# Packed constant loads, contiguous input and output, and a new order of the first and last stage

## The reference

```
x = x + layernorm(mamba(layernorm(x)))       # in-projection, convolution, scan over 16 states, out-projection
x = x + layernorm(moe(layernorm(x)))         # 8 experts, top 2 of a softmax, and a shared ninth expert
x = x + layernorm(diff_attention(layernorm(x)))   # 8 heads, difference of two softmaxes, RMS norm
x = x + layernorm(ffn(layernorm(x)))         # attention whose q, k, v and output matrices are mixed from
                                             # 8 experts by a gate of each row, then a mixture of 8 experts
```

## Time and profile before

| what | us |
|---|---|
| median of 3 runs | 2786.39 |
| lowest and highest of them | 2784.11, 2788.78 |
| span of the profiled execution | 2789.0 |
| busy: PE | 2152.8 |
| busy: DVE | 2099.8 |
| busy: ACT | 1749.7 |
| busy: POOL | 1545.8 |
| share of the last chain on PE, DVE, ACT, issue, POOL | 34%, 30%, 12%, 12%, 11% |

### The profile page before, as it was taken

One profiled execution on the slowest core, in us unless ns is written; L12 is line 12 of the kernel. 1 busy time (PEld: TensorE's weight loads), 2 busy tenths in 40 slices (PEclk: granted clock), 3 DMA queues, 4 the chain that ended last, 5 costly groups with the idle time before them and its releaser, 6 DMA issues.

```text
span 2789.0 us, 42437 instructions
## 1 busy us (share of the span) xinstructions
PE 2152.8 (77%) x15570; PEld 1465.2 (53%) x15570; DVE 2099.8 (75%) x3549; ACT 1749.7 (63%) x2757; POOL 1545.8 (55%) x1375
## 2 busy tenths in 40 slices
PE   2333787588499597989889888989896699659876
PEld 1101455256266474655566566656664568546665
DVE  3999889789888315999999999999998531762344
ACT  5444776686575545988888888888894234222432
POOL 0435433533534103878877887888787524464146
PEclk8555898799599798999999999999997799879988
DMA  3000000000000000100000000111010000000000
GB/s 109 0 0 0 1 1 1 1 1 1 19 1 1 12 12 20 28 24 24 24 24 24 24 24 24 25 31 28 24 35 22 2 1 1 1 16 1 1 1 16
DMA packets 32033, 42.07 MB, mean 15 GB/s; under 512 B 8897, under 2 KB 18130, under 8 KB 31442
## 3 DMA queue, kind: packets, MB, share of 16 engines
q1 hardware_dynamic: 31826, 39.34, 5.2%
HBM read 12.05 MB, written 2.10 MB: 5 GB/s over the span
## 4 chain that ended last, share of the span: by engine, by line
PE 34%; DVE 30%; ACT 12%; issue 12%; POOL 11%; SPq 0%; DMA 0%; POOLq 0%; ACTq 0%; DVEq 0%
DVE MA L1330 12%; PE ps L892 6%; DVE WB L1339 5%; POOL MA L430 3%; PE ps L821 3%; ACT HR L793 2%; PE ps L1162 2%; PE ps L823 2%; PE ps L822 2%; PE ps L1191 2%; PE ps L2064 2%; ACT BIG L464 2%; PE ps L1174 2%; PE ps L2006 1%; ACT L793 1%
## 5 line engine op out<-in xcount | busy, mean ns | idle before, releaser
L1330 DVE TENSOR_REDUCE MA<-ps 128x1 f32<-128x1024 f32 x512 | 606.5, 1215 | 46.6 <-PE ps L1162 42.6
L1258 ACT ACTIVATE WB<-ps,MA 128x1024 f32<-128x1024 f32 x461 | 513.4, 1117 | 105.8 <-DVE MA L1330 93.5
L430 POOL TENSOR_TENSOR MA<-MA,BIG 128x1024 f32<-128x1024 f32 x128 | 303.0, 2389 | 494.9 <-DVE BIG L356 470.4
L1162 PE MATMUL ps<-BIG 96*128 96x512 f16 x1024 | 316.0, 391 | 98.7 <-ACT WB L1258 87.2
L1414 POOL TENSOR_SCALAR WB<-WB,MA 128x384 f32<-128x384 f32 x256 | 371.1, 1450 | 8.5
L892 PEld LDWEIGHTS ps<-WB,HR 128*128 128x128 f32 x2304 | 278.9, 195 | 27.4 <-issue 11.6
L892 PE MATMUL ps<-WB,HR 128*128 128x128 f32 x2304 | 285.9, 280 | 7.2 <-DVE acc L728 7.2
L793 ACT ACTIVATE HR<-ps,b 128x512 f32<-128x512 f32 x288 | 190.2, 686 | 127.7 <-PE ps L823 126.6
L1782 POOL TENSOR_TENSOR BIG<-MA,BIG 128x512 f32<-128x512 f32 x128 | 132.7, 1048 | 228.6 <-PE ps L2050 74.3
L1174 PE MATMUL ps<-ident,WB 128*128 128x128 f32 x1640 | 223.8, 280 | 9.8 <-DVE WB L1339 5.7
L1417 POOL TENSOR_TENSOR WB<-WB 128x384 f32<-128x384 f32 x205 | 208.9, 1019 | 17.1
(11 more groups left out here) (314 smaller groups left out, 4959.8 us busy)
## 6 DMA issues: line engine op xcount, KB each, us to landing
BIG<-BIG SPq DMA_DIRECT2D x192, 64.0 KB, 2.0
BIG<-MA SPq DMA_DIRECT2D x192, 64.0 KB, 2.0
WB<-w_dram SPq DMA_DIRECT2D x1, 2304.0 KB, 14.8
X<-x_dram SPq DMA_DIRECT2D x4, 512.0 KB, 12.5
HR<-w_dram SPq DMA_DIRECT2D x1, 2048.0 KB, 9.6
out_dram<-X SPq DMA_DIRECT2D x4, 512.0 KB, 3.2
BIG<-wqkv_dram SPq DMA_DIRECT2D x1, 1536.0 KB, 6.2
WB<-w_dram SPq DMA_DIRECT2D x2, 512.0 KB, 5.1
```

The costliest lines, as they stand in the source:

```text
L430: e.tensor_tensor(yy[:, c, :], yy[:, c, :], db[n % 2][c], ALU.add).then_inc(*p_my.up(b, n, c))
L1162: x = e.matmul(ps[s][:, 512 * h:512 * h + 512], stack[q % 2][0:96, 0, 2 * pp + s, 128 * i:128 * i + 128], stack[q % 2][0:96, 1, 2 * pp + s ...
L1258: e.activation(P_of(n, s), ps[s][:, :], ACT.Exp, bias=L[:, 2 * s + pp:2 * s + pp + 1], scale=1.0, accum_out=L[:, 4 + 2 * s + pp:5 + 2 * s ...
L1330: e.tensor_reduce(L_of(n)[:, c:c + 1], ps[s][:, :], AX, ALU.max, negate=True).then_inc(*v_amx.up(n, s))
```

## The change

Three things change together.

First, the loads. The host packs nine constants side by side into one array `first` of 128 x 1148 and ten others into `second` of 128 x 725 (values that were broadcast on the chip are now repeated on the host), and lays x out so that a partition's eight tiles lie in one row. SP issues x of batch 0, `first` and `second`, then the rest as before. `first` counts on `s_c`, `second` on a new semaphore `s_c2`. The output is stored in the same contiguous layout, and the host puts it back.

Second, the prologue. Selector block 1 goes from ACT to DVE, both of DVE's blocks come after the statistics instead of before them, and tiles 4 to 7 of batch 0 are normalized on DVE (new semaphore `v_mln`), tiles 0 to 3 on ACT.

Third, all the tables have new numbers, so instructions of the first stage, of the attention's edges and of the last stage stand in another order. The 256 units of the attention keep theirs.

```diff
+FIRST = (("ident", 128), ("winT", 512), ("convw", 6), ("convb", 2), ("bdt", 2), ("dcol", 2), ("alog", 32), ("wx", 208),
+         ("wdt", 256))
+SECOND = (("gwT", 8), ("b1", 36), ("gam", 1), ("sims", 16), ("woT", 256), ("iota8", 8), ("tri", 128), ("lam", 128),
+          ("gts", 16), ("b2", 128))
...
-OUT_AT = {"gate": 6.85, "yy": 4.84, "out": 11.16, "stats": 19.32, "rstd": 21.7, "norm": 32.4, "x": 35.2}
+OUT_AT = {'gate': 6.46, 'yy': 8.89, 'out': 9.57, 'stats': 16.28, 'rstd': 18.81, 'norm': 30.44, 'x': 35.17}
...
-        a_const = Tick(sem("a_const"), keys(("alog", "sel0", "sel1"), )  + keys(("w1",), 9) + [("gw",)])
-        v_const = Tick(sem("v_const"), keys(("aneg", "sel2"), ) + keys(("w1",), 9) + [("gw",), ("ones",)])
+        a_const = Tick(sem("a_const"), keys(("alog", "sel0"), )  + keys(("w1",), 9) + [("gw",)])
+        v_const = Tick(sem("v_const"), keys(("sel1", "sel2", "aneg"), ) + keys(("w1",), 9) + [("gw",), ("ones",)])
+        v_mln = tick("v_mln", ("in",))
...
         def const_act(e):
-            e.wait_ge(s_c, S_C)
...
+            e.wait_ge(s_c, 16)
+            e.activation(aneg[:, :], packed["alog"], ACT.Exp, bias=0.0, scale=1.0).then_inc(*a_const.up("alog"))
+            e.activation(*selected(0), ACT.Copy, scale=1.0).then_inc(*a_const.up("sel0"))
...
         def const_dve(e):
+            yield IN_AT0["stats"] + 1
+            e.wait_ge(s_c, 16)
+            for k in (1, 2):
+                e.tensor_copy(*selected(k)).then_inc(*v_const.up(f"sel{k}"))
+            yield IN_AT0["norm"] + 1
             e.wait_ge(*a_const.at("alog"))
             e.tensor_scalar(aneg[:, :], aneg[:, :], -1.0, None, ALU.mult).then_inc(*v_const.up("aneg"))
...
+            if b == 0:
+                yield in_at(b, "norm")
+                e.wait_ge(*p_mrs.at(b, "in"))
+                norms(e, st["m"], [tile_of(b, j) for j in range(8)], lnb[0], range(4, 8)).then_inc(*v_mln.up("in"))
...
         def load(e):
-            e.dma_start(X[:, 0:8, :], xin[:, 0:8, :]).then_inc(s_x[0], 16)
-            for dst, src in consts:
-                e.dma_start(dst, src).then_inc(s_c, 16)
+            def rows_of(b):
+                return X[:, 8 * b:8 * b + 8, :].rearrange("p j c -> p (j c)"), d["x"][128 * b:128 * b + 128, :]
+
+            e.dma_start(*rows_of(0)).then_inc(s_x[0], 16)
+            e.dma_start(head_[:, :], d["first"]).then_inc(s_c, 16)
+            e.dma_start(rest_[:, :], d["second"]).then_inc(s_c2, 16)
...
-                e.dma_start(ov[:, 8 * b:8 * b + 8, :], X[:, 8 * b:8 * b + 8, :]).then_inc(s_o, 16)
+                e.dma_start(out[128 * b:128 * b + 128, :], X[:, 8 * b:8 * b + 8, :].rearrange("p j c -> p (j c)")).then_inc(
+                    s_o, 16)
```

167 lines of the change are left out of this document (72 added, 95 removed), and 6 rows, old and new, of the table D_AT.

## The result

The changed kernel takes 2716.41 us (median of 4 runs, 2715.46 to 2722.15) against 2787.23 (median of 4, 2784.11 to 2788.78): 0.9751 of the time, 95% interval 0.9737 to 0.9764. The span of the profiled execution went from 2789.0 to 2713.5, 75.5 us less.

What follows compares the result with a forecast made beforehand. It took DVE to bound the scan, with bare chains in prologue, transition and last stage; 12.2 + 1 + 5 + 5.8 + 2.3 + 0.4 = 26.7 us off 2789.0, less 2.6 to the median, gives 2759.7, range 2746 to 2773.

Steps and rivals of the forecast that it cites:

- the term of the first stage: First stage, batches beside the scan: the new order takes 1 us off, between 6.8 off and 6.4 more.
- the statistics' move: First stage, DVE: out-projection statistics one scan (2.27 us) earlier, so X is ready earlier; up to 6.8 us off.
- the wait for the taps: First stage: first taps stand later on ACT, so DVE waits up to 3.2 us more in two batches, 6.4 together.
- The order pays in full: Rival, chance 0.10: transition gives 10 us, first stage 5, all else as summed; 35.7 off, 2750.7 us.
- The loads: Prologue: X lands at about 4.3 us, `first` at 6.6, first transpose at 15.7 instead of 27.90; gain 12.2 us.
- The blocked case: Prologue: DVE's selector copies hold up POOL, statistics come 4.5 us later; gain 12.2 us instead of 15.7.
- the crowding rival: Rival, chance 0.09: X and `first` land only with HR at 12 us; prologue gives 7.5 us with blocking, 2764.4.
- The transition: From attention to last stage: three DVE idle times, 16.2 us together, shrink; 5 us off, between 0 and 10.
- Behind the projection: Last stage: sums and statistics leave the bare DVE and POOL chain; 5.8 us off in round 0, 2.3 in round 1.
- PE's total is as before, so the end of unit b is too: Last stage's output projection: steps stay 1.33 us when a unit runs alone, so unit b ends no later.
- The slower case: Rival, chance 0.04: projection by single units takes 1.95 us a step, 40 us more in 64 steps; 2799 us.
- The store: Output: last store gains 0.4 us from longer rows, between 0 and 0.8.

Runs made afterwards that it cites:

- the kernel with the later copies: The changed kernel with DVE's two selector copies behind its four normalization tiles instead of ahead of them; median 2715.25 us over 9 runs.
- the five kernels with single keys: Each the changed kernel with part of IN_AT or OUT_AT as before: first taps 2724.03, DVE's taps 2746.0, exponentials 2731.22, statistics 2724.81, products 2721.78 us.

## Why the prediction was wrong

**The step that failed is the term of the first stage.** It was put at -1 us, with ends at -6.8 and +6.4; the scan part became 34 to 40 us shorter than in the trace of before. It failed in four ways.

The reach was wrong. The prediction looked at the first stage in one window, 73 to 285 us, in which DVE is busy 206.4 of 212.0, and concluded that DVE sets the pace and an order can't bring much. That window holds batch 0's 16 steps and the first few of batch 1. It is the part without experts: their first product runs at 291.5 us. The same view for the rest tells another story:

```profile
75.10:287.10 212.00, 77.00 (x158) 21.59 (x158) 206.14 (x186) 90.71 (x108) 100.86 (x52) 0.56 0.00 0
287.10:890.10 603.00, 470.57 (x2759) 309.15 (x2760) 517.96 (x723) 425.98 (x537) 244.18 (x124) 0.88 0.01 3
```

In the 603 us that follow DVE is idle 85.0, and by its waits it stands behind PE and ACT. DVE's busy time hardly changed (724.1 us in the 64 steps, then 721.9), so the gain is idle time. This was in the trace of before. The honest upper end for a new order of this stage was those 85 us, and not the two waits of the earlier trace rows that had an obvious partner in the diff.

The reading of the waits was wrong. The prediction says that what little DVE waits, it waits for ACT and POOL. The view of those rows, 520 to 750 us, has this above them:

```profile
DVE acc L728 <- PE ps L892: 13.8, 7, 3.9
```

DVE's largest wait was for PE, twice the 6.5 for X that was priced. The sum had no term for it, and it fell by 9 to 14.6 us over the 64 steps. Of ACT's, the 9.4 for `xT` went, also without a term.

The method was wrong. Two moves were priced (the statistics and the taps) and the remaining new numbers taken as neutral. The moves that matter are others: the exponentials against the gelus, the experts' gate and loop against the scans. And the two that were priced have the wrong price: the statistics' move is worth nothing measurable, and the wait for the taps, put at up to 6.4 more, became 4.4 less.

The premise that an order's parts can be priced one by one is doubtful itself. Undone tables cost 8 to 37 us each, and the costs of the experts' and the projections' tables add up to twice what undoing all of them costs. What bounds the whole is the idle time of the pacing engine.

**No rival covered it.** "The order pays in full" came nearest, with 5 us for the first stage and 2750.7, for the same reason.

**What held, by its own steps:**

- The loads: X at 4.27 (forecast 4.3), transpose at 15.23 (15.7), gain 12.6 (12.2). The blocked case was right, and the kernel with the later copies shows that they are its cause. `first` came a microsecond earlier than forecast (in the 19 traces with the new loads X landed 3.55 to 4.30 us after its issue). The lower end of that term was to be halfway to HR's figure, which is 3.0 us later and gives 9.2, not 9.5; nothing rested on it. HR's transfer of 2048 KB did not push the two ahead of it back, so the crowding rival is out; the Trainium skill, DMA: Bandwidth & Descriptors, section Queues, rings and completion order, says that an engine takes one queue's descriptors in order, and the trace agrees: X landed 3.55 us after its issue, HR in 9.6.
- The transition: 5 forecast; 3.3, and 3.3 more in the attention's last units. The range from 0 to 10 was right, all three idle times went, and two shorter ones (2.55 and 2.78) came.
- Behind the projection: round 0 became 5.7 us shorter (5.8 forecast) and round 1 2.2 (2.3; 19.2 to 17.0 from the last sum to the gate). The step "PE's total is as before, so the end of unit b is too" did not hold: from the first transpose to unit b's sum each round takes 43.9 us instead of 42.8. Each unit starts with a step of 1.85 us, and the change of units takes 2.28, where before every step behind the first was 1.33. Round 1 loses another 0.5 ahead of the projection, so that from its first gate to its second it is only 0.5 us shorter. What stands ahead of round 0's projection (-2.5), its experts (-2.6) and the tail (-1.2) were not in the sum and bring the last stage to 11.5 instead of 8.1. That the number came near is in part luck.
- The slower case, a projection at 1.95 us a step, did not come: 1.33 within a unit, as the two buffers say.
- The store: 0.6, 0.4 forecast.
- From span to median: the prediction took 2.6 us off, the difference in before. For the changed kernel the median is 2.9 above the profiled span. These 5.5 us are the difference between 48.8 (spans) and 43.3 (medians) of error. The 2.6 were no property of the kernel: a run's time lies 1.8 to 2.6 us above its own span everywhere, and before's profiled execution was a slow one.

**The attention's rest.** Of its 7.2 us, 3.9 are neither transition nor order, as its units stand in the same order. In the traces here that stretch took between 1035.7 and 1043.3 us. In the changed kernel's three traces it was 1036.1, 1037.4 and 1037.4. Before's 1043.3, the longest, stands in the slow execution; the kernel with the loads alone, whose order there is before's, took 1039.6. The mean granted clock was 0.98 in before and the changed kernel alike. What moves this stretch, and whether the change has a part in it, stays open.

**Still open:** what `LOOP_AT` is worth alone, which tables must match which beyond the places shown, and so how much of the 34 to 40 us each holds.

## What to carry to other kernels

Before pricing a new order, take the idle time of the engine that sets the pace in every stage, stage by stage, and use it as the end of the range. A window with the lightest load beside the pacing engine says nothing of the others. Read the list of waits from its top. Count as priced only what has been traced, and leave the rest its full width: where tables are matched, undoing one can make an order that neither kernel had, and its loss is then not what the table was worth.

Where a constant's preparation is moved from one engine to another, look at who shares a path with the new engine at that moment. Here two copies of 2.3 us on DVE held up two small POOL instructions by 4.1 us, and standing one step later they held up nothing.

An experiment on one key of such a table is only clean where the order shows that one engine alone moved (four of the five kernels with single keys); else its trace, not its time, is the result.

## What the runs showed of the hardware

- The same kernel's 64 scan steps took 777.9, 783.2 and 784.4 us, with PE busy 541.9, 552.3 and 553.8 us at granted clocks of 0.81, 0.79 and 0.79. Nearly all of it is seen as DVE's wait for PE at `acc`, 26.9, 32.4 and 32.5 us; its other waits are the same to a microsecond. Effects under 6 us can't be read from one trace of this kernel.
- POOL beside a copy on DVE with one input: 2.34 and 3.66 us instead of 0.25 and 1.67. Before, only the scan, with two inputs, had been seen to do this.
- A load of 512 KB landed 3.55 us after its issue (to 4.30 in other traces), with three others, 3.0 MB together, issued within 1.4 us behind it.
